# A graph layer on one core: the order of the one-hots before the blanks, of the keys and values in the second convolution, and of the general way's dummy row

## The reference, cut to what matters

```python
xn = layernorm(x)
def conv(h):                      # twice: conv(conv(xn W1) W2)
    return segment_sum((h @ W)[src] * weight[:, None], dst)
k, v = layernorm_per_head(xn @ wk.T), layernorm_per_head(xn @ wv.T)   # 4 heads of 64
kv = einsum('sd,se->de', k, v) / N            # a sum over all nodes, per head
x1 = x + conv2(xn) + ((xn @ wq.T) @ kv) @ wo.T + bo
y  = layernorm(x1)
out = x1 + ffn(y)                 # gate of 16 experts, top 2, then layer norm
```

## Time and profile before

| | us |
|---|---|
| median of 3 runs (3553.7 to 3566.8) | 3566.45 |
| the profiled execution's own time | 3555.0 |
| its span | 3553.3 |

### The profile page before, as it was taken

The page is one execution under the profiler, slowest core; times in us unless marked ns, Lnnn a source line. Parts: engine busy times, 40 slices in busy tenths (PEclk is TensorE's granted clock), DMA queues, the critical chain, the costliest instruction groups (busy, mean ns, idle before and its releaser), DMA issues.

```text
span 3553.3 us, 48849 instructions
## 1 busy us (share of the span) xinstructions
PE 2837.9 (80%) x14428; PEld 2004.0 (56%) x14429; DVE 1397.2 (39%) x3864; ACT 1375.1 (39%) x2993; POOL 1939.6 (55%) x2028
## 2 busy tenths in 40 slices
PE   1899989989999997888887888788867648999930
PEld 0566656656655664555555555555546547878820
DVE  8455545555555553322222222122225641111157
ACT  4687777767777672000000000000004423333322
POOL 2666665655656564466666666666643651222235
PEclk9899999999999998898889998888888869999975
DMA  6344434434444444655555555555532334443454
GB/s 218 120 158 157 158 122 154 158 122 151 157 151 128 152 158 152 214 162 163 162 162 161 161 170 163 154 168 156 163 94 84 117 125 133 139 155 124 125 153 123
DMA packets 268800, 528.11 MB, mean 149 GB/s; under 512 B 58951, under 2 KB 155214, under 8 KB 268480
## 3 DMA queue, kind: packets, MB, share of 16 engines
q0 software_dynamic: 89232, 242.05, 22.8%
q1 hardware_dynamic: 148256, 252.66, 21.6%
q10 hardware_dynamic: 31120, 31.04, 2.7%
HBM read 395.21 MB, written 131.79 MB: 148 GB/s over the span
## 4 chain that ended last, share of the span: by engine, by line
PE 57%; issue 12%; ACT 11%; another core or an unknown queue 7%; DVE 6%; DMA 4%; SPq 2%; POOL 0%; ACTq 0%; DVEq 0%; POOLq 0%
PE bank L964 25%; PE bank L952 9%; PE sums L977 5%; PE bank L1187 4%; ACT build L760 3%; ACT build L762 3%; DMA pa<-ys_d 3%; PE bank L1042 3%; PE bank L1175 2%; PE bank L987 2%; ACT pa L767 1%; PE sums L935 1%; PE bank L996 1%; PE bank L935 1%
## 5 line engine op out<-in xcount | busy, mean ns | idle before, releaser
L655 POOL DMA_INDIRECT pa<-xn_d,srcs x816 | 786.7, 964 | 511.8 <-PE sums L977 300.5
L655 POOL DMA_INDIRECT pa<-h_d,srcs x816 | 796.9, 977 | 420.0 <-issue 228.5
L964 PE MATMUL bank<-t1s,pa 128*128 128x256 f32 x2450 | 644.8, 409 | 113.9 <-issue 103.5
L964 PEld LDWEIGHTS bank<-t1s,pa 128*128 128x128 f32 x2450 | 489.6, 205 | 266.6 <-issue 196.6
L952 PE MATMUL bank<-build 128*128 128x343 f32 x1500 | 503.7, 475 | 129.2 <-DVE build L1347 59.6
L964 PE MATMUL bank<-t0s,pa 128*128 128x256 f32 x2450 | 555.7, 383 | 5.4 <-DVE pa L1365 4.6
L1365 DVE TENSOR_TENSOR pa<-bank,pa 128x343 f32 x750 | 376.0, 513 | 410.4 <-ACT pa L767 187.5
L964 PEld LDWEIGHTS bank<-t0s,pa 128*128 128x128 f32 x2450 | 459.4, 190 | 102.4 <-issue 42.6
L952 PEld LDWEIGHTS bank<-build 128*128 128x128 f32 x1500 | 272.5, 194 | 336.0 <-issue 264.6
L762 ACT ACTIVATE build<-build,ones 128x343 f32<-128x343 f32 x750 | 436.2, 582 | 24.4
L760 ACT ACTIVATE build<-build,tabs 128x343 f32<-128x343 f32 x750 | 424.8, 566 | 31.0 <-issue 26.1
(11 more groups left out here) (256 smaller groups left out, 2622.1 us busy)
## 6 DMA issues: line engine op xcount, KB each, us to landing
slab_d<-pa SPq DMA_DIRECT2D x175, 448.0 KB
pa<-slab_d SPq DMA_DIRECT2D x175, 448.0 KB
pa<-in_w ACTq DMA_DIRECT2D x32, 512.0 KB, 4.2
pa<-in_w SPq DMA_DIRECT2D x32, 512.0 KB, 3.6
pa<-ys_d SPq DMA_DIRECT2D x109, 130.0 KB
pa<-xn_d,srcs POOLq DMA_INDIRECT x816
pa<-h_d,srcs POOLq DMA_INDIRECT x816
pa<-eo_d SPq DMA_DIRECT2D x49, 256.0 KB, 3.1
```

The source lines that it names most:

```text
L655: pool.indirect_dma_start(gath[g % RING * QT + j], None, table, bass.IndirectOffsetOnAxis(ap=srcs[:, n:n + 1], axis=0)).then_inc(s_g[g % R ...
L964: ins = pe.matmul(app[:, 0:D], slab3[:, s, :], table[:, s * D:(s + 1) * D], start=s == 0, stop=s == T - 1)
```

## The change

It does four things.

1. EARLY_MV goes from 14 to 18 (all MR buffers). Eight of these one-hots stand ahead of the blank of plane 0, two ahead of each of planes 1 to 5, none ahead of plane 6. LR and EARLY_LO go from 24 to 23.
2. The keys and values get two buffers of `xT` and `kvn` (the squares go into `kvn`), and their steps new planes: for odd tiles `kv_in` at plane 5 of the unit before, `kv_proj` at 1, norm at 3, `kv_sum` at 6; for even ones 1, 4, 6 and 2 of the next unit. Unit 0 has its own order for three tiles. Since `kvm` has one bank, `kv_proj` now waits for the scaling of the tile before (`s_m_r`).
3. FG goes from 8 to 4. POOL loads the row's three tables before it waits for the last step, `fcol` is gone, and PE and DVE read `first`, `n_rows` and `steps` ahead of the last placings.
4. `s_acc2` is given ahead of the small memsets, and SP waits for the last plane instead of `s_acc2` before it loads the next stage's rows.

```diff
-LR = 24
+LR = 23
-EARLY_LO = 24
-EARLY_MV = 14
+EARLY_LO = 23
+EARLY_MV = 18
-FG = 8
-FR = NCH // FG
+FG = 4
+FR = -(-E // (FG * P))
...
+        PROJ0 = {1: 0, 3: 1, 5: 2}
+        def proj_at(i, p):
+            if i == 0:
+                return PROJ0.get(p)
+            return {1: 2 * i + 1, 4: 2 * i + 2}.get(p) if i < KVT else None
+        def turn_at(i, p):
+            if i == 0 and p < 5:
+                return {0: 0, 1: 1, 3: 2}.get(p)
+            return {5: proj_at(i + 1, 1), 1: proj_at(i, 4)}.get(p)
+        def norm_at(i, p):
+            return proj_at(i, p - 1) if i == 0 else proj_at(i, p - 2)
+        def sum_at(i, p):
+            if i == 0:
+                return {4: 0, 6: 1}.get(p)
+            if i == 1 and p == 0:
+                return 2
+            return {6: proj_at(i, 1), 2: proj_at(i - 1, 4) if i > 1 else None}.get(p)
...
 # SP, second convolution
-                    if kv_of(i) == KV:
-                        if p == 0:
-                            xn_load(i * KV + 1, 1)
-                        if p == 3:
-                            sp.wait_ge(s_m_tp, i * KV + 1)
-                            xn_load(i * KV + 2, 0)
-            sp.wait_ge(s_acc2, 1)
+                    u = turn_at(i, p)
+                    if u is not None and u + 2 < T:
+                        sp.wait_ge(s_m_tp, u + 1)
+                        xn_load(u + 2, u % 2)
+            sp.wait_ge(s_ap, 2 * CT * NU)
...
 # POOL, all_rows
-                pool.wait_ge(s_hu, STEPS * (layer + 1))
                 with pool.Fori(0, n_rows) as j:
...
                     pool.wait_ge(s_fi, (n_rows + j + 1 if layer else j + 1) * 48)
+                    pool.wait_ge(s_hu, STEPS * (layer + 1))
...
 # ACT, first convolution
-                        for m in range(p * 2, min(EARLY_MV, (p + 1) * 2)):
+                        for m in range(8 + 2 * (p - 1) if p else 0, min(EARLY_MV, 8 + 2 * p)):
                             moving(i + 1, m)
                         blanks(i, p)
...
 # PE
+            first, n_rows = first_row(pe)
+            steps = total(pe)
             place_gathered(GU - 1, 0)
             place_dense(NU - 1, 0)
-            all_rows(0)
+            all_rows(0, first, n_rows, steps)
             def kv_proj(u):
                 pe.wait_ge(s_m_xT, u + 1)
-                pe.wait_ge(s_wkv, 1)
+                if u == 0:
+                    pe.wait_ge(s_wkv, 1)
+                else:
+                    pe.wait_ge(s_m_r, (u - 1) * 5 + 3)
...
 # DVE
-            ext_rows = ext[0:1, :, :].rearrange("o (g c) m -> o g c m", c=FG)
+            ext_rows = ext[0:1, 0:FR * FG, :].rearrange("o (g c) m -> o g c m", c=FG)
-            link(dve.tensor_scalar(fcol[:], fcol[:], float(NCH - FG), None, ALU.min))
...
             dve.wait_ge(s_ap, 2 * CT * NU)
+            mark(s_acc2)
             link(dve.memset(y3[:, :, D:RW], 0.0))
             link(dve.tensor_copy(y3[:, :, D], tok[:]))
             link(dve.memset(yk[:, :, D:RW], 0.0))
-            mark(s_acc2)
```

More of the change, by code:

```diff
@@ L74 @@
 MMC = NCH // MMP
[L75 removed]
+assert EP >= E and 2 * DG == NCH and MMP * MMC == NCH and (FR + 1) * FG == NCH
 KV = 2
 KVT = (T - 1) // KV
[L78 removed]
+assert KV * KVT + 1 == T and KVT == NU - 1
 assert KB % 2 == 0 and EARLY_LO <= LR and EARLY_MV <= MR and QK % HK == 0 and FG * P <= HB * HK * P
@@ L666, in all_rows @@
                     pool.nop(nofuse=True)
-                    at = pool.value_load(cols(fcol, r, 1), min_val=0, max_val=NCH - FG)
+                    at = nc.s_assert_within(r * FG, 0, NCH - FG, skip_runtime_bounds_check_because="it is a row's")
                     for to, given in ((fsrc, src_t), (fdst, dst_t), (fwt, wt_t)):
@@ L820, in _ @@
             for i in range(NU):
-                u, kv = i * KV, kv_of(i)
                 for p in range(CT):
[L823 to L832, removed]
+                    if norm_at(i, p) is not None:
+                        squares(norm_at(i, p))
+                        roots(norm_at(i, p))
+                    if turn_at(i, p) is not None:
+                        turned(turn_at(i, p))
                     takes(steps_at(i, "p", p, 1), 1)
@@ L1004, in all_gathered, with all_rows @@
                         place_gathered(s // QK - 1, layer)
-            def all_rows(layer):
-                first, n_rows = first_row(pe)
-                steps = total(pe)
+            def all_rows(layer, first, n_rows, steps):
                 with pe.Fori(0, n_rows) as j:
@@ L1039, in kv_proj @@
                 pe.wait_ge(s_m_xT, u + 1)
-                pe.wait_ge(s_wkv, 1)
+                if u == 0:
+                    pe.wait_ge(s_wkv, 1)
+                else:
+                    pe.wait_ge(s_m_r, (u - 1) * 5 + 3)
                 for a in range(2):
-                    ins = pe.matmul(kvm, xT[:, a, :], wkv[:, a, :], start=a == 0, stop=a == 1)
+                    ins = pe.matmul(kvm, xT[u % 2][:, a, :], wkv[:, a, :], start=a == 0, stop=a == 1)
                 ins.then_inc(s_m_mm, 1)
@@ L1047, in kv_sum @@
                 pe.wait_ge(s_m_kvn, u + 1)
+                kn = kvn[u % 2]
                 for p in range(2):
-                    ins = pe.matmul(kvs[:, p * P:(p + 1) * P], kvn[0:m, D + p * P:D + (p + 1) * P],
-                                    kvn[0:m, p * P:(p + 1) * P], start=u == 0 and p == 0, stop=False,
+                    ins = pe.matmul(kvs[:, p * P:(p + 1) * P], kn[0:m, D + p * P:D + (p + 1) * P],
+                                    kn[0:m, p * P:(p + 1) * P], start=u == 0 and p == 0, stop=False,
                                     skip_group_check=True)
@@ L1076, in _ @@
                     all_gathered(steps_at(i, "p", p, 1), 1)
[L1077 to L1080, removed]
+                    if sum_at(i, p) is not None:
+                        kv_sum(sum_at(i, p))
+                    if proj_at(i, p) is not None:
+                        kv_proj(proj_at(i, p))
+                    if turn_at(i, p) is not None:
+                        kv_in(turn_at(i, p))
                     if p == 4 and i == KVT:
                         mix_in()
[L1083 to L1088, removed]
                     if p == 6 and i == KVT:
                         mix_out()
-                    if p == 6 and kv == KV:
-                        kv_sum(u + 1)
             place_gathered(GU - 1, 1)
             place_dense(NU - 1, 1)
-            all_rows(1)
+            all_rows(1, first, n_rows, steps)
             pe.wait_ge(s_wc, 3)
@@ L1422, in all_gathered, with all_rows @@
                         place_add(0, s // QK - 1, table)
-            def all_rows(layer, table):
-                first, n_rows = first_row(dve)
-                steps = total(dve)
+            def all_rows(layer, table, first, n_rows, steps):
                 dve.wait_ge(s_hu, (layer + 1) * STEPS)
@@ L1482, in _ @@
                               ).then_inc(s_wkv, 1)
+            first, n_rows = first_row(dve)
+            steps = total(dve)
             place_add(0, GU - 1, t1s)
             place_add(1, GU + NU - 1, t1s)
-            all_rows(0, t1s)
+            all_rows(0, t1s, first, n_rows, steps)
             mark(s_acc)
@@ L1538, in _ @@
                         place_add(1, GU + i - 1, t0s)
+                    if norm_at(i, p) is not None:
+                        kv_vars(norm_at(i, p))
+                        kv_norm(norm_at(i, p))
+                    if p == 3:
+                        dense_hots(i, 1)
                     if p == 4 and i == KVT:
                         mix_in()
-                    if p == 1 and kv:
-                        kv_vars(u)
-                        kv_norm(u)
                     if p == 5 and i == KVT:
                         mix_mid()
-                    if p == 3:
-                        dense_hots(i, 1)
-                    if p == 4 and kv == KV:
-                        kv_vars(u + 1)
-                        kv_norm(u + 1)
                     if p == 6 and i == KVT:
@@ L1554, in _ @@
             place_add(1, GU + NU - 1, t0s)
-            all_rows(1, t0s)
+            all_rows(1, t0s, first, n_rows, steps)
             dve.wait_ge(s_ap, 2 * CT * NU)
+            mark(s_acc2)
             link(dve.memset(y3[:, :, D:RW], 0.0))
```

44 lines of the change are left out of this document (21 added, 23 removed).

## The result

The changed kernel takes 3534.33 us (median of 5), the kernel before 3563.64 (5): ratio 0.9921, 95% interval 0.990 to 0.9942. The forecast was 3466 with a range of 3410 to 3530. So 29 us came of the 100 that the sum gave. The profiled execution has a span of 3536.4 us, 16.9 less than that of before.

What follows compares the result with a forecast made beforehand. The prediction took PE to bound both convolutions. Gains of 31 (rows), 17 (one-hots) and 52 us (keys and values) made 100: 3555 - 100 = 3455, plus 11.4 to the median, 3466; range 3410 to 3530.

Steps and rivals of the forecast that it cites:

- Step 1: Dummy rows behind both convolutions: 14.4 us gained each, 3.5 at the next stage's loads, 1 lost in preparation; 31.3 together.
- Part 1: The same forecast for the dummy rows, points 3 and 4 of the change: 31.3 us gained.
- Step 2: First convolution: more one-hots ahead of the blanks cut PE's waits for ACT (13.2 us) and DVE (6); 17 us net.
- Part 2: The same forecast for the one-hots, point 1 of the change: 17 us gained.
- Step 3: Second convolution: new planes for keys and values gain 32 us of hand-overs, 17 of clock, 3 of DVE and ACT; 52.
- All four checks: Second convolution: PE's hand-over waits under 10 us, clock over 0.90, POOL's full-ring idle near 90, stage near 1160.
- 32 us of hand-overs: Second convolution: of PE's 40 us idle before L1042 and L1049, all but a fifth goes.
- The second term, 17 us of clock: Second convolution: fewer long waits spare some ten projections a slow-clock loss of 1.7 us each; 17 us.
- A: Second convolution: PE is short of instructions and fills the freed time with that; median 3513, chance 0.24.
- B: Second convolution: slower, as PE's new wait in kv_proj costs 6 us at each of 23 even tiles; 3695, chance 0.05.
- C: Second convolution: PE is freed wholly and POOL becomes the bound; median 3385, chance 0.08.

Runs made afterwards that it cites:

- row_only: The kernel before with only the two dummy rows shortened, their loads earlier, and LR and EARLY_LO at 23; 3243.13 us, ratio 0.9895 on a prompt device.
- two_tiles_only: row_only with 47 of the 49 tiles of keys and values left out; 3529.3 us, ratio 0.9892 on a late device.
- before_again: The kernel before, unchanged, run again for its trace, on a late device; one execution of 3567.8 us.
- row_and_onehots: row_only with the new order of the one-hots and EARLY_MV at 18; 3245.36 us, ratio 0.9893 on a prompt device.

## Why the prediction was wrong where it was

**Step 1, the dummy row: right.** 13.8 us against 14.4 in the first, 16.1 against 14.4 + 3.5 in the second, 1.2 lost in the preparation against 1. The gathers sat where the sum put them, and the one-hots on DVE did not become the bound. Eight matmul records took 3.77 us, not 3.05. Part 1 is the whole measured gain: row_only gives all of it on a prompt device (0.9895) without the rest.

**Step 2, the one-hots: wrong, 17 us forecast, none seen.** The first half happened. PE's waits for ACT ahead of the dense placing fell from 13.2 to 5.6 us. The waits behind it grew instead (waits of PE in the changed kernel, 80 to 1400):

```profile
PE bank L972 <- DVE pa L1383: 24.1, 15, 9.9
...
PE bank L984 <- DVE pa L1383: 8.5, 14, 1.6
...
PE bank L1016 <- ACT ob L808: 5.6, 10, 0.7
```

I had halved the 11.7 us for DVE; they doubled. The step that failed is "the blank comes up to 2.2 us earlier". With its one-hots gone, the last blank waited for the plane's signal instead, as here:

```profile
666.80 5.34 PE L984 MATMUL bank<-t0s,pa 128*128 128x256 f32 x24
...
667.90 0.58 ACT L785 ACTIVATE build<-build,ones 128x343 f32<-128x343 f32 x1
669.15 0.95 ACT L790 ACTIVATE pa<-zero 128x896 f32<-128x896 f32 x1 [0.67 <-issue]
...
673.86 0.95 ACT L790 ACTIVATE pa<-zero 128x896 f32<-128x896 f32 x1 [3.75 <-remote]
674.71 0.36 ACT L808 ACTIVATE ob<-bank 128x256 f32<-128x256 f32 x1
674.94 0.52 DVE L1383 TENSOR_TENSOR pa<-bank,pa 128x343 f32 x1 [9.43 <-ACT pa L790]
```

The plane's last matmul ended at 672.14, ACT was free from 670.1, and the blank began at 673.86. Over 24 units the blanks are done 2.6 us after the last plane, against 2.9 before and 1.0 on a prompt device with either order. The check "blank 6 within 1 us of the last plane's end" was thus not met on average: the blanks came 0.3 us earlier, not up to 2.2. Part 2 by itself was run on a prompt device alone, so on a late one the 17 us are answered by the trace only; its first convolution is 3.6 us longer, and that is less than the 13 us between two executions of one kernel. The earlier trace rows also left out the largest of PE's waits inside the stage (kernel before):

```profile
PE bank L952 <- issue: 48.0, 55, 9.8
```

**Step 3, keys and values: wrong, 52 us forecast, 8 lost in the trace.** All four checks failed: 28 us of waits instead of under 10, clock 0.87 instead of over 0.90, ring waits 139.6 instead of 90, stage 1216 instead of 1160. What failed is the sentence "so PE paces it". The rows had the limit in them: 1025 us of gathers with their gaps and 33.1 until h_d is there leave about 153 of the 1211 us, 140.2 of them "remote" waits. A gain had to come out of these, whatever PE waited for. I took them as proof that PE's work was behind. A full ring says only that the consumer's signal has not come, and where POOL waited, PE's own record of the step had ended 8.9 us earlier on average. With 104 us of PE's work taken away (two_tiles_only) the stage stayed at 1216 us. The 32 us of hand-overs were also too many for the rows: of the 40 us that they are a share of, 17.4 stand under "issue", where PE waited for no hand-over, so 22.6 were there to be had. The remark on the earlier trace rows (squares up to 14.9 us after PE's record, "with nothing seen in between") was, by its "remote" label, most likely the same thing, read as a loss local to ACT. The second term, 17 us of clock, hung on fewer waits and fell with them.

**The rivals.** A came nearest in time (3513) and had the right direction: the freed time was filled again. What it was to show itself by, more than 140 us of "issue" at the planes, did not come: they are 73.9, after 103.5 before. A tenth fewer matmuls in two_tiles_only changed nothing in the stage either, so the number of instructions does not set it; what the "issue" waits of PE on a late device are stays open. On a prompt device the 96 packets of instructions are the same and PE's idle time ahead of a plane of the second convolution is 1.6 us; there the Trainium skill's statement ("Runtime: NRT & Kernel Launch", Instruction fetch mechanics) that fetching is mostly hidden agrees with the trace. B's waits in `kv_proj` were 9.8 us (for L1521 and L1524), far from its 2.9 us a tile. C named the right engine and the wrong consequence: on a prompt device POOL is the bound already before PE is freed (row_only), and on a late one its gathers set the stage together with late signals.

## What to carry to other kernels

Add up what the producer cannot give up (its work, usual gaps and start) before asking which engine is busiest. What is left of the stage bounds any gain, and the question is then what the rest waits for. When a consumer's record ends long before its producer goes on, the ring is waiting for a signal and not for work, and a new order of the consumer's other jobs need not help; whether more slots would was not measured where signals are late. Test it by leaving the suspected work out altogether: if the stage does not move without it, little can be hoped from reordering it.

## What the runs showed of the hardware

Two Trainium2 chips need not be alike for such a kernel: 3563 us on one, 3278 to 3282 on four others, with the same instructions and bytes and the same length of a gather (958 to 977 ns in all traces). The difference lies in the two convolutions (1325.6 and 1210.1 us in before_again, against 1182.9 and 1063.5 in row_only) and goes with the lag of PE's semaphore increments: over 1 us for 229 of 379 planes and steps of the second convolution in before_again, for none in row_only and one in row_and_onehots. In the turn shown above the held-up increments arrived within 0.3 us of each other. The traces of the two kinds also differ in how many increments they record at all, of DMAs and of every engine: some 27,000 on late chips (27,134 before, 26,869 after), some 53,600 on prompt ones (53,647 in row_only), for nearly the same program. Whether increments were merged on the way or only not recorded, the traces don't say. A gain that depends on such waits can differ by device as well. That of the rows (0.9885 to 0.9895 on prompt chips, 0.9921 and 0.9892 on late ones with it included) does not clearly: the intervals overlap. No chip was seen in both kinds, but only one of them was met twice (a prompt one), so whether the kind belongs to the chip or to something else about those runs is open too.
